# Ordering the edges with one-hots of eight columns per operation, and a shorter mish

## The reference

```python
h = relu(layernorm(x)); x = x + (concat([h, mean_of_neighbours(h)]) @ W0.T + b0)
h = relu(layernorm(x)); x = x + rel_conv1(relu(rel_conv0(h)))    # 8 relations, 4 bases, edge_weight
h = relu(layernorm(x)); x = x + message_pass(h, edge_attr_4, edge_attr_8)
h = relu(layernorm(x))
m = mish(mish(concat([h[src], h[dst], edge_attr_64]) @ W1 + b1) @ W2 + b2)    # once per edge
agg = segment_sum(m, dst)
x = x + layernorm(h + mish(concat([h, agg]) @ W3 + b3) @ W4 + b4) * gamma + beta
```

## Time and profile before

| | us |
|---|---|
| three runs | 2323.88, 2331.24, 2334.01 |
| median of them | 2331.24 |
| profiled execution, its own time | 2325.94 |
| its span | 2324.2 |
| TensorE busy | 2038.3 (88%) |
| VectorE busy | 1774.2 (76%) |
| ScalarE busy | 1456.0 (63%) |
| GpSimd busy | 1291.8 (56%) |

### The profile page before, as it was taken

One profiled execution on the slowest core, in us unless ns is written; L12 is line 12 of the kernel. 1 busy time (PEld: TensorE's weight loads), 2 busy tenths in 40 slices (PEclk: granted clock), 3 DMA queues, 4 the chain that ended last, 5 costly groups with the idle time before them and its releaser, 6 DMA issues. The chain is left out here.

```text
span 2324.2 us, 36961 instructions
## 1 busy us (share of the span) xinstructions
PE 2038.3 (88%) x11455; PEld 1106.1 (48%) x11455; DVE 1774.2 (76%) x3095; ACT 1456.0 (63%) x2429; POOL 1291.8 (56%) x1065
## 2 busy tenths in 40 slices
PE   0787688789988949999999987999999999999865
PEld 0433577546655624444444453455555554555422
DVE  8999899853333348888888853999999999999723
ACT  1999777421122225555555534999999999999822
POOL 0576677518810034444444204788888888888530
PEclk9999999989989969999999999999999999999988
DMA  2410100112143244333333304232222222222000
GB/s 114 165 27 14 55 0 0 59 32 78 41 123 98 83 139 142 93 100 99 95 93 95 71 16 134 87 92 76 77 74 76 75 74 74 77 70 78 10 0 22
DMA packets 81562, 170.33 MB, mean 73 GB/s; under 512 B 17378, under 2 KB 43221, under 8 KB 80449
## 3 DMA queue, kind: packets, MB, share of 16 engines
q0 software_dynamic: 35840, 98.88, 15.6%
q1 hardware_dynamic: 45624, 70.25, 9.1%
HBM read 144.93 MB, written 23.98 MB: 73 GB/s over the span
## 5 line engine op out<-in xcount | busy, mean ns | idle before, releaser
L884 PE MATMUL e_two_ps<-w,e_first 128*128 128x512 bf16 x1408 | 419.8, 380 | 0.1
L1629 ACT ACTIVATE u_msg<-u_t,slot_record 128x128 f32<-128x128 f32 x704 | 223.3, 390 | 98.0 <-DVE u_t L1685 97.9
L643 POOL DMA_INDIRECT sorted_records<-edge_record,slot_row x160 | 209.9, 1312 | 123.6 <-issue 57.8
L884 PE MATMUL e_two_ps<-w,e_first_low 128*128 128x512 bf16 x704 | 267.3, 380 | 0.0
L1813 POOL TENSOR_TENSOR e_first_low<-e_first 128x1024 bf16<-128x1024 f32 x88 | 250.1, 2842 | 21.9 <-DVE e_first L2004 21.9
L1818 POOL TENSOR_TENSOR e_msg_low<-e_act 128x1024 bf16<-128x1024 f32 x88 | 225.6, 2563 | 55.9 <-DVE e_act L2016 54.7
L1547 POOL DMA_INDIRECT u_got<-up_table,u_idx x176 | 185.0, 1051 | 76.8 <-issue 43.7
L2309 POOL DMA_INDIRECT e_got<-src_table,e_idx x176 | 186.6, 1060 | 70.5 <-issue 35.5
L884 PEld LDWEIGHTS e_two_ps<-w,e_first 128*128 128x128 bf16 x1408 | 134.4, 98 | 148.6 <-issue 2.2
L685 PE MATMUL pairs_ps<-cell_high,src_hot 128*128 128x144 bf16 x1180 | 153.0, 227 | 44.5 <-POOL cell_rest L709 22.4
L1593 PE MATMUL u_sum_ps<-u_msg,u_hot 128*125 128x512 f32 x352 | 185.1, 608 | 7.5 <-ACT u_msg L1629 7.5
(11 more groups left out here) (366 smaller groups left out, 5140.6 us busy)
## 6 DMA issues: line engine op xcount, KB each, us to landing
conv_w<-in_L_gnn_basis_dram SPq DMA_DIRECT2D x8, 1024.0 KB
sorted_records<-pairs SPq DMA_DIRECT2D x5, 1408.0 KB, 10.9
edge_record<-in_edge_floats_dram SPq DMA_DIRECT2D x2, 3125.0 KB
later_w<-in_L_gnn_W_dram SPq DMA_DIRECT2D x6, 1024.0 KB
attr_parts<-h SPq DMA_DIRECT2D x22, 256.0 KB, 2.1
e_attrT<-attr_parts SPq DMA_DIRECT2D x44, 128.0 KB
e_dst_all<-dst_row SPq DMA_DIRECT2D x44, 125.0 KB
pairs<-in_edge_floats_dram SPq DMA_DIRECT2D x1, 3125.0 KB
```

Source lines behind the costliest of these rows:

```text
L643: pg.nc.gpsimd.indirect_dma_start(out=pg.sorted, out_offset=bass.IndirectOffsetOnAxis(ap=pg.slot_row[:, j:j + 1], axis=0), in_=pg.edge_rec ...
L884: last = nc.tensor.matmul(out, lhsT, rhs, start=(n == 0), stop=(n == len(pairs) - 1))
L1629: last = nc.scalar.activation(msg[:, k, at * MUL:(at + 1) * MUL], t12[:, k % 2, of], ACT.Copy, scale=pg.record[:, bass.ds(t, 1), Y + m])
```

## The change

Ordering works on batches of eight columns (BATCH), 20 of them, with two buffers. One-hots are laid out with the column innermost, so that VectorE makes each kind for eight columns in one tensor_tensor: lanes (1024 values per partition), tiles (1888), two key parts (2048) and two weight parts (2048), all of 16-bit types, against a table `iota_eights` that constants() fills (1888 values). The third weight part stays with ScalarE, as eight scaled copies per batch, which read the lanes at a step of eight values. TensorE's products are the same 40 per eight columns; it reads the tile one-hot and four of the five stationary operands at a step of eight values (16 bytes). The buffers lie in the last 4960 floats of `pairs`, which GpSimd clears after `placed`; it clears the first 12800 before its scatters, and ScalarE the rest in 16 pieces of 690 floats.

The first half of the records is scattered as 52 columns during ordering and 28 in layer0 (5 before the bias is awaited, 23 behind the bias additions). The second half is loaded as 52 columns in build_pairs and 28 at the end of layer0, where SP waits for all 80 scatters and ScalarE for that load before it copies names; conv 0 scatters those 80 as before.

In the edge pass, mish is Exp, then (x + 2) * x on VectorE in place of the clamp, then Ln with a scale and a bias, then Exp: the two squares per unit are gone from ScalarE. TensorE reads the destination rows straight from the table, at a register that it loads in every first_layer; `block_rows` is gone. L1981 becomes a tensor_tensor against a table that edge_tables fills on GpSimd, and the four L1987 of a group become one operation.

```diff
+FIRST = 52
+BATCH = 8
...
+LOG_SCALE = 0.75 * 2.0 ** -64
+LOG_BIAS = 2.0 * LOG_SCALE
+SHARE_BIAS = float(np.log(2.0) + np.log(LOG_SCALE))
...
+    pg.iota_eights = pg.hT[:, :, :].rearrange("p f n -> p (f n)")[:, PT:PT + PT * BATCH // 2].bitcast(BF16)\
+        .rearrange("p (t j) -> p t j", j=BATCH)
...
+            nc.gpsimd.iota(pg.iota_eights[:, :, :], [[1, PT], [0, BATCH]], base=0, channel_multiplier=0,
...
+            for ends, at in ((pg.edge_record[0:EP, 0:EARLY, SRC:SRC + 2], slice(0, EARLY)),
+                             (pg.late_ends, slice(EARLY, EARLY + FIRST)), (pg.last_ends, slice(EARLY + FIRST, EC))):
...
+        lane_hot = pg.sb("pair_lane_hot", [EP, 2, P, BATCH], BF16, ctx)
+        BATCHES, WAITED = EC // BATCH, 4
...
+        weight_hot = pairs[0:EP, HOTS:HOTS + 2 * P * BATCH].bitcast(BF16).rearrange("p (s c l j) -> p s c l j", s=2, c=2, l=P)
+        rest_hot = pairs[0:EP, HOTS + 2 * P * BATCH:HOTS + 3 * P * BATCH].bitcast(BF16)\
+            .rearrange("p (s j l) -> p s j l", s=2, j=BATCH)
+        tile_hot = pairs[0:EP, HOTS + 3 * P * BATCH:].bitcast(BF16).rearrange("p (s t j) -> p s t j", s=2, j=BATCH)
...
+            nc.gpsimd.memset(pairs[:, 0:CLEARED], 0.0)
             pool.wait_ge(pg.emptied, 16 * 5)
-            scatter_records(pg, range(0, EARLY))
-            pool.wait_ge(decoded, 1)
-            pairs = pg.pairs[:, :, :, :].rearrange("p s n d -> p (s n d)")
-            size = pairs.shape[1] // 4
-            for n in range(1, 4):
-                nc.gpsimd.memset(pairs[:, n * size:(n + 1) * size], 0.0)
+            scatter_records(pg, range(0, FIRST))
+            pool.wait_ge(placed, 1)
+            nc.gpsimd.memset(pairs[:, HOTS:], 0.0)
...
-            for i in range(EC // STRIDE):
-                for n in range(STRIDE):
-                    s = n % 4
-                    pe.wait_ge(keys_hot, STRIDE * i + n + 1)
+            for i in range(BATCHES):
+                s = i % 2
+                pe.wait_ge(keys_hot, i + 1)
+                for j in range(BATCH):
                     for c in range(2):
-                        nc.tensor.matmul(column(c), key_hot[:, s, c, :], tile_hot[:, s, :], start=False, stop=False)
-                    pe.wait_ge(weights_hot, STRIDE * i + n + 1)
-                    for c in range(3):
-                        last = nc.tensor.matmul(column(2 + c), weight_hot[:, s, c, :], tile_hot[:, s, :],
-                                                start=False, stop=False)
-                    last.then_inc(free, 1)
+                        nc.tensor.matmul(column(c), key_hot[:, s, c, :, j], tile_hot[:, s, :, j], start=False, stop=False)
+                pe.wait_ge(weights_hot, i + 1)
+                for j in range(BATCH):
+                    for c in range(2):
+                        nc.tensor.matmul(column(2 + c), weight_hot[:, s, c, :, j], tile_hot[:, s, :, j],
+                                         start=False, stop=False)
+                pe.wait_ge(rests_hot, i + 1)
+                for j in range(BATCH):
+                    last = nc.tensor.matmul(column(4), rest_hot[:, s, j, :], tile_hot[:, s, :, j],
+                                            start=False, stop=False)
+                last.then_inc(free, 1)
...
-                    for c in range(3):
-                        last = nc.scalar.activation(weight_hot[:, s, c, :], lane_hot[:, s, :], ACT.Copy,
-                                                    scale=pg.weight_part[:, c, bass.ds(j, 1)])
-                    last.then_inc(weights_hot, 1)
-            act.wait_ge(pg.emptied, 16 * 5)
-            pairs = pg.pairs[:, :, :, :].rearrange("p s n d -> p (s n d)")
-            size = pairs.shape[1] // 4
-            nc.scalar.activation(pairs[:, 0:size], pg.ones[:, 0:1].broadcast_to([P, size]), ACT.Copy, scale=0.0)
+            size = (HOTS - CLEARED) // (BATCHES - WAITED)
+            for i in range(BATCHES):
+                act.wait_ge(lanes_hot, i + 1)
+                act.wait_ge(free, i + 1)
+                for j in range(BATCH):
+                    last = nc.scalar.activation(rest_hot[:, i % 2, j, :], lane_hot[:, i % 2, :, j], ACT.Copy,
+                                                scale=pg.weight_part[:, 2, bass.ds(BATCH * i + j, 1)])
+                last.then_inc(rests_hot, 1)
+                if i >= WAITED:
+                    act.wait_ge(pg.emptied, 16 * 5)
+                    at = CLEARED + (i - WAITED) * size
+                    to = pairs[:, at:at + size]
+                    nc.scalar.activation(to, pg.ones[:, 0:1].broadcast_to(list(to.shape)), ACT.Copy, scale=0.0)
...
-                    nc.vector.tensor_scalar(lane_hot[:, s, :], pg.iota_lane[0:EP, 0:P],
-                                            pg.pair_lane[:, bass.ds(j, 1)], None, ALU.is_equal).then_inc(lanes_hot, 1)
-                    nc.vector.tensor_scalar(tile_hot[:, s, :], pg.iota_lane[0:EP, :],
-                                            pg.pair_tile[:, bass.ds(j, 1)], None, ALU.is_equal)
-                    for c in range(2):
-                        last = nc.vector.tensor_scalar(key_hot[:, s, c, :], pg.iota_lane[0:EP, 0:P],
-                                                       pg.pair_lane[:, bass.ds(j, 1)], pg.key_part[:, c, bass.ds(j, 1)],
-                                                       ALU.is_equal, ALU.mult)
-                    last.then_inc(keys_hot, 1)
...
+            for i in range(BATCHES):
+                s = i % 2
+                at = slice(BATCH * i, BATCH * (i + 1))
+                dve.wait_ge(free, i + 1)
+                nc.vector.tensor_tensor(lane_hot[:, s, :, :], pg.iota_eights[0:EP, 0:P, :], over(pg.pair_lane[:, at], P),
+                                        ALU.is_equal).then_inc(lanes_hot, 1)
+                nc.vector.tensor_tensor(tile_hot[:, s, :, :], pg.iota_eights[0:EP, :, :], over(pg.pair_tile[:, at], PT),
+                                        ALU.is_equal)
+                dve.wait_ge(lanes_hot, i + 1)
+                lanes = lane_hot[:, s, :, :].rearrange("p (a l) j -> p a l j", a=1).broadcast_to([EP, 2, P, BATCH])
+                nc.vector.tensor_tensor(key_hot[:, s, :, :, :], lanes, parts(pg.key_part[:, :, at]),
+                                        ALU.mult).then_inc(keys_hot, 1)
+                nc.vector.tensor_tensor(weight_hot[:, s, :, :, :], lanes, parts(pg.weight_16[:, :, at]),
+                                        ALU.mult).then_inc(weights_hot, 1)
...
+def late_records(pg, sp, begin, end):
+
+    sp.dma_start(pg.edge_record[0:EP, begin:end, :],
+                 pg.inp["edge_floats"].rearrange("(p j) r -> p j r", j=EC)[:, EARLY + begin:EARLY + end, :])\
+        .then_inc(pg.record_in, 16)
+
+
+def name_ends(pg, begin, ends):
+
+    for n, column in enumerate((SRC, DST)):
+        pg.nc.scalar.copy(pg.edge_record[0:EP, begin:begin + ends.shape[1], column], ends[:, :, n])
...
-            sp.wait_ge(pg.scattered, 16 * EARLY)
-            sp.dma_start(pg.edge_record[0:EP, 0:EC - EARLY, :],
-                         pg.inp["edge_floats"].rearrange("(p j) r -> p j r", j=EC)[:, EARLY:EC, :])\
-                .then_inc(pg.record_in, 16)
+            sp.wait_ge(pg.scattered, 16 * FIRST)
+            late_records(pg, sp, 0, FIRST)
...
+            sp.wait_ge(pg.scattered, 16 * EARLY)
+            late_records(pg, sp, FIRST, EARLY)
...
+            act.wait_ge(pg.record_in, 32)
+            name_ends(pg, FIRST, pg.last_ends)
...
+            scatter_records(pg, range(FIRST, FIRST + 5))
             pool.wait_ge(bias_in, 16)
             for b in range(NB):
                 nc.gpsimd.tensor_tensor(pg.x[:, b, :], pg.x[:, b, :], bias[:, :], ALU.add).then_inc(biased, 1)
+            scatter_records(pg, range(FIRST + 5, EARLY))
...
+                pool.wait_ge(pg.record_in, 32)
...
+                at = nc.tensor.value_load(pg.block_of_group[0:1, bass.ds(g, 1)], min_val=0, max_val=NB - 1)
...
-                    nc.tensor.matmul(ps, dst_part[:, h, 0, cols], hotT[:, h, :], start=True, stop=False)
-                    nc.tensor.matmul(ps, dst_part[:, h, 1, cols], hotT[:, h, :], start=False, stop=False)
+                    for part in range(2):
+                        rows = by_dst[:, bass.ds(at, 1), part, cols].rearrange("p b d -> p (b d)")
+                        nc.tensor.matmul(ps, rows, hotT[:, h, :], start=(part == 0), stop=False)
...
-            def square1(n, u):
-                act.wait_ge(clamped1, n + 1)
-                nc.scalar.activation(act1[:, u, :, :], act1[:, u, :, :], ACT.Square,
-                                     bias=pg.ones[:, 0:1]).then_inc(act1_chain, 1)
...
+                act.wait_ge(widened1, n + 1)
+                nc.scalar.activation(act1[:, u, :, :], act1[:, u, :, :], ACT.Ln, scale=LOG_SCALE,
+                                     bias=pg.log_bias[:, 0:1]).then_inc(logged1, 1)
...
-                square2(n, u)
                 log2(n, u)
                 if more:
-                    square1(n + AHEAD, u)
```

(60 more changed lines are left out.)

98 lines of the change are left out of this document (41 added, 57 removed).

## The result

| | before | changed | ratio (95% interval) |
|---|---|---|---|
| median, us | 2331.21 | 2546.71 | 1.0936 (1.0918 to 1.0953) |
| span of the profiled execution, us | 2324.2 | 2545.0 | |

The kernel became 215 us slower, where 39 us faster was forecast, and the time lies far outside the range. The profiled executions differ by 220.8 us of span. Read from the first instruction of each stage, that is shared out as follows.

What follows compares the result with a forecast made beforehand. Ordering was taken as bound by VectorE and ScalarE together, the edge pass by TensorE. Terms -52 + 1.9 - 1 + 19 - 7 = -39 give 2286.8 us profiled, 2292 as median; range 2262 to 2345.

Steps and rivals of the forecast that it cites:

- first term of the loop: Ordering loop, TensorE: 40 products per batch take 4.04 us, if reads at a step of 16 bytes cost nothing.
- rival (a): Ordering: strided reads slow TensorE, which becomes the bound; 2364 us at double time, 2335 at 1.65 times; chance 0.14.
- VectorE's batch: Ordering loop, VectorE: four operations on 7008 elements take 3.95 us per batch, 4.4 with what scatters take.
- ScalarE's strided copy: Ordering loop, ScalarE: 0.42 us per strided scaled copy, 3.4 for eight, 4.2 per batch with the clear.
- The loop: Ordering, 20 batches at 4.5 us: 90 us against 142.1, so -52; bounds 82 to 106 us.
- Layer0: layer0, price of splitting the records: later scatters, second load and name copies add 19 us (+8 to +26).
- Constants: constants(), filling the 1888 elements of iota_eights: +1.9 us, bounds 0 to 2.5.
- Decode: Decode after the ordering loop: loses sharing with the 18 us memset, gets scatters beside it; -1 us (0 to -3).
- Edge pass: Edge pass: shorter chains and removed VectorE work cut TensorE's waits; -7 us (-12 to 0).
- Rival (c): Edge pass: value_load on TensorE isn't hidden, 88 x 0.77 = 68 us, time 2360 us; chance 0.06.
- Rival (b): Ordering: tensor_tensor at L306's rate, 7.5 + 0.45 us per batch, loop 159 us, time 2361 us; chance 0.05.
- Rival (d): Ordering: back-to-back tensor_tensors starve scatters, 2.6 us or more each; build_pairs starts later, +25, 2317 us; chance 0.08.

Runs made afterwards that it cites:

- e1: Changed kernel with only the tile one-hot's values side by side again, made by one tensor_scalar per column; 2313.76 us, ratio to before 0.9945.
- e7: e1 with the second load behind conv 0's first weights, names copied in conv 0, a 1024-wide constants table, first three tile batches by tensor_tensor; 2290.71 us, ratio 0.9859.
- e9: e4 with the one-hots of destinations made by tensor_scalar as before; one run of 2317.77 us.
- e4: Kernel before with the edge pass of the change alone, ordering and records as before; 2318.9 us, ratio 0.9964.
- e3: Changed kernel with batches of two columns instead of eight, strided reads at 4 bytes; one run of 2353.03 us.
- e2: Changed kernel with batches of four columns instead of eight, strided reads at 8 bytes; one run of 2371.5 us.

## Why the prediction was wrong

**The step that failed** is the first term of the loop: "8 x 0.505 = 4.04 us per batch, if the reads at a step of 16 bytes cost nothing". It measured 16.85. The prediction knew that no row had such a read, gave no bound for it in the sum, and took the free end for the forecast. The bound came only as rival (a), whose mechanism is what happened: TensorE became the bound, VectorE waited for buffers, and the kernel is slower. But it had a chance of 0.14 and was priced at double time at most, 2364, with nothing in the rows behind the factor two; 4.2 times was measured. With a range that is to take in the bounds of unknown costs, an operand with no row near it needed a price in proportion to the step: 16 bytes against 2, up to eight times. By the table above it is four, because up to 4 bytes are free.

**What held.**
- VectorE's batch: 3.92 us against 3.95. The 0.55 ns per element was a choice between two bounds, twice the lower one, and it came out. The 0.45 us per batch that scatters were to take from VectorE didn't show in its tensor_tensors: with scatters beside them in e1 (157.51 to 162.10) they took 0.60, 1.14 and 1.13 us from start to start, as in the changed kernel before its first scatter (0.60, 1.13 and 1.13).
- ScalarE's strided copy: eight of them stand 3.40 us ahead of the next operation in e1's timeline (107.78 to 111.18), 0.425 from start to start (0.42 forecast).
- The loop, had the tile one-hot lain side by side: 90 forecast, 102.6 in e1 and 93.2 in e7. That 93.2 is near 90 is partly luck, since eight tensor_scalars (1.72 us) stand there for one tensor_tensor (1.06), about as much more as the scatters' 0.45 that didn't show. The 9.4 between e1 and e7 is the memset's hold on VectorE, which the prediction called hidden: it looked only at who waits behind the memset on GpSimd, and not at who shares something with it.
- Layer0: +24.6 against +19 (+8 to +26). The holds by the four L964 were there, at 4.5 to 4.9 us per scatter instead of 4.35, and three of 2.3 to 2.8 among the first five; the load took 10.7 from issue to the names instead of 9.7. The forecast's own terms give 505.8 for the last scatter and not 505.
- Constants: +3.3 against +1.9, outside its bounds. The iota with a repeated inner step took 1.83 ns per element and not the 1.06 of the row that it was sized by.
- Decode +0.7 against -1, build_pairs +0.2, conv 0 nothing. In the decode one tensor_scalar was held by the second memset for 2.6 us, which the forecast didn't have.
- Edge pass: -7.7 against -7. Waits for the low part 20.4 to 16.8 (-3.6, forecast -3.6 with the last unit's), for e_first 6.3 to 4.0 (-2.3, as forecast), for the first product 6.2 to 5.1 (-1.1, forecast -1.2). Rival (c) is out: with 88 value_loads TensorE was busy 399.25 of 400 us in mid-pass. But the longest wait of the last unit stayed at 5.0 us, and the one behind it went from 3.1 to 2.0. So the gain there is that of the very last mish.

**What isn't explained by the change**: the tail, +3.6 us with the same instructions. In the profiled executions from the last product of the edge pass to the end it is 99.2 us before, 102.8 in the changed kernel, and between 99.5 and 102.8 in the experiments, e9 (100.0) and e4 (102.6) among them. In the slower ones, more of the groups of eight products of the tail took 5.37 or 6.37 us instead of 3.67, in stretches with a lower granted clock (0.83 on average over 2503 to 2523 us of the changed kernel, 1.00 over the like stretch of before). It follows no edit here.

Rival (b) is out by the 3.92 us. Rival (a) names 6.3 us per batch as the point where the gain is gone; by its own sum it is (90 + 39) / 20 = 6.45, which changes nothing here. Rival (d) didn't decide in the changed kernel, as VectorE mostly waited there, but it did in e3.

## What to carry to other kernels

A layout that lets one engine make eight things at once has to be paid by the engine that reads them: size the reader first, and where no row has its access pattern, bound the price by the step (bytes passed over), not by a factor that feels large. Lay the moving operand of a product side by side; a stationary one could be strided up to 16 bytes here, because its loads lay beside products. And when work is moved beside other work, look at pairs of engines as well as at queues: here a memset held tensor_scalars, and tensor_tensors held indirect DMAs, and neither shows as a wait in the profile, only as a long instruction.

## What the runs showed of the hardware

- TensorE's moving operand of bf16: 0.44 to 0.46 ns per column at steps of 2 and 4 bytes, 0.91 at 8, 1.78 at 16, all at a granted clock of 1.00.
- Weight loads of 128 columns: 145 ns with a step of 16 bytes (e1), 117 with 8 (e2), 97 and 98 with 4 (e3) and 97 side by side.
- GpSimd's memset of 12800 floats (10.8 us) stopped VectorE's 16-bit tensor_scalars until it ended (11.70 us for 1.78 us of work), and let its tensor_tensors pass. The memset of 4960 floats did so to a tensor_scalar of 236 values (2.89 us for 0.28). In the kernel before, a tensor_scalar of 5 elements (L626) took 2.7 us until the end of its memset; the prediction made no use of that line.
- VectorE's tensor_tensors from SBUF, back to back, kept one indirect DMA of GpSimd from ending for 85 us.
- The 16-bit tensor_tensor with both operands at step one innermost took 0.55 ns per element (1.13 us from start to start for 2048), and one with an operand repeated innermost 1.08 (2.03 for 1888). The Trainium skill's page "VectorE: DVE Perf Modes" ("The perf-mode tier table") has two elements per cycle for the former, an estimate of 3.65 us and the starts for a batch; it agrees with the 3.92 measured.
